# LSTM and three sign-weight layers on one core: more steps under the seven products, and low parts computed in pieces between the recurrence's instructions

## The chip, the core and the metric

One core of a Trainium2 chip. The metric is the device time of one execution in microseconds (us), median of several. TensorE multiplies into PSUM; ScalarE, VectorE and GpSimd do the elementwise work; SyncE and ScalarE issue the DMAs.

## The reference, cut to what matters

```python
# x (32, 64, 256): batch 32, 64 steps; h0 = cond_1024 (32, 256); c0 = 0
xW = x @ Wx + b                                   # (32, 64, 1024)
for t in range(64):
    a = xW[:, t] + h @ Wh                         # i, f, o, g of 256 each
    c = sigmoid(f) * c + sigmoid(i) * tanh(g)
    h = sigmoid(o) * tanh(c);  hs[:, t] = h
y = concatenate([hs, -hs], -1)
y = relu(s0 * (y @ sign(k0))) * 2                 # 512 -> 1024, weights +1 or -1
y = relu(s1 * (y @ sign(k1))) * 2                 # 1024 -> 1024
out = x + s2 * (y @ sign(k2))                     # 1024 -> 256
```

## The kernel before

Values are held transposed: features on the 128 partitions, steps times batch in columns. Precision comes from pairs: a value is a 16-bit high part and a 16-bit low part (value minus high part), and each product is two matmuls, one for each part.

**The recurrence.** In step t TensorE adds 16 matmuls of 32 columns (L512, high part of h) and 16 of 64 columns (L521, both parts) to the three gate sums. VectorE adds the halves (`add_halves`, L965: forget gate, then input gate and candidate, then output gate), ScalarE takes the tanh of each (L717), VectorE makes uT (L1063), vT (L1066), cD (L1069) and oP (L1071), ScalarE tanh of the cell (L834), and VectorE h's high part (L1075), h in 32 bits (L1076) and its low part hl (L1078). Between, ScalarE seeds the next step's gate sums from xw (L710). Each engine runs its instructions in program order.

**The filler.** All other matmuls are put by `make_plan` behind the gate matmuls of some step, in the order of `tile_order`, each step with a budget in us (`fill`). A tile is an output of 128 features: ("x", i, j) is input projection (six 512-column f32 matmuls, L542), (0, c, n) and (1, c, n) are tiles of the first and second layer for portion c (4 and 16 matmuls, L559), ("o", c, k) the third layer's four matmuls on the second layer's tile k (L592). `CHUNKS` gives portions as first step and number of steps, 32 columns a step: five of 8 and two of 12.

**Emptying a tile.** ScalarE writes the high part (`layer_hi`, L733) or, for x, adds the bias and stores to xw (`x_empty`, L701), behind the seeds of the next step (`act_plan`). VectorE writes the low part (`layer_lo`, L888), behind hl and ahead of the next step's gate sums (`dve_plan`). The planner counts them as emptied, and later matmuls really wait for the semaphores.

**The last two portions, N1 and N2,** share the second layer by Winograd's form of Strassen's algorithm: seven half-size products p1 to p7 of NW columns (L577) in place of eight, with sums of weights (`mix_part`, GpSimd, L1136) and of activations. For N1's first-layer tiles ScalarE writes a 32-bit copy r1 (L727) and then the high part (L733), and GpSimd the low part (`r1_rest`, L1156). p1 and p2 run within the steps; ScalarE empties them (`p1_copy` L738, `c11_hi` L743), VectorE writes p2's low part (`c11_lo`, L893). Behind the last step come N2's first layer with its four VectorE operations a block (`n2_terms`, L917 to L922), the third layer of portion N1 - 1 interleaved (`tail_order`), its two adds (L903), the third layer's first half for N1 (L612), which waits for these adds, then p3 to p7, and the remaining outputs, adds and stores. Splits of x into high and low parts sit in fixed steps (`X2_STEPS`, `X3_STEPS`; `x_hi` at L692).

The core of the planner's choice for VectorE:

```python
time = ahead + STEP + spent - CHAIN - KEEP - LOW * (t in W2_STEPS)
for x in todo:
    if len(now) < 2 or sum(map(vector_cost, now + [x])) <= time:
        now.append(x)
```

`todo` are finished tiles whose last matmul lies at least 0.75 us (planned) ahead of the step's end, and older ones.

Of the kernel before, what the change touches and what calls it, by code (L numbers as in the profile page):

```python
# [37 lines left out]
CHUNKS = ((0, 8), (8, 8), (16, 8), (24, 8), (32, 8), (40, 12), (52, 12))  # L38
N1, N2 = 5, 6
# [17 lines left out]
CHORES, EVICTIONS = 1.3, 1.7  # L57
# [41 lines left out]
def act_cost(tile):  # L99
    return 0.48 if tile[0] == "y" else 0.67 if tile[0] == "x" else 0.95 if tile[:2] == (0, N1) else 0.38  # L100


# [49 lines left out]
def make_plan():  # L152
# [124 lines left out]
    for tile, a in tail_order(rest):  # L277
# [7 lines left out]
        if a + 1 == matmuls(tile) and tile[0] in (0, 1, "p2", "p3", "p4", "p7"):  # L285
            free.append((bank[tile], tile))
            empty_at[tile] = at + 1.2
            if tile[0] == 0:
# [4 lines left out]


def lstm_ffn(nc, x_d, small_d, wx_d, wh_d, k0_d, k1_d, k2_d, out_d):
    ctx = ExitStack()
    with ctx:
# [918 lines left out]
```

## Time and profile before

| | |
|---|---|
| median of 3 runs | 272.74 us (272.41 to 273.35) |
| the profiled execution | 272.65 us, its span 270.7 us |
| TensorE busy | 266.5 us, 98% |
| VectorE busy | 219.5 us, 81% |
| ScalarE busy | 193.0 us, 71% |
| GpSimd busy | 48.2 us, 18% |
| granted TensorE clock | 0.999 |

A busy TensorE counts overlapping matmuls once; a listed duration of one matmul is longer than the distance to the next, so pitches are read from runs of equal matmuls in a row. Lines are numbered as in the kernel printed above; L559 and its like are the matmuls of the layers.

### The profile page before, as it was taken

The numbers are of one execution on the slowest core, as the hardware profiler recorded it, in microseconds if no ns is written. First come the engines' busy times: TensorE is split into PE (matmuls) and PEld (weight loads), VectorE is DVE, ScalarE is ACT, GpSimd is POOL, SyncE is SP. The second block draws the span as 40 slices with busy tenths as digits, with TensorE's granted clock in tenths as the row PEclk, the third lists the DMA queues.
The fourth block names the chain that finished last, engine by engine and source line by source line (L and its number), as shares of the span: only waits on it lengthen the run. The fifth ranks groups of instructions, "written<-read, shape, count | busy, mean of one in ns | idle before, by whom it ended". The sixth has DMA issues, their size and how long they took to land.

```text
span 270.7 us, 9163 instructions
## 1 busy us (share of the span) xinstructions
PE 266.5 (98%) x3568; PEld 220.0 (81%) x3568; DVE 219.5 (81%) x833; ACT 193.0 (71%) x650; POOL 48.2 (18%) x70
## 2 busy tenths in 40 slices
PE   8999999999999999999999999999999999999995
PEld 5877888888999999999999999998887777556663
DVE  3887888888888888888888888888887777998355
ACT  5799898989677768766867677667888976734320
POOL 0010000022211112331222102000222225603030
PEclk9999999999999999999999999999999999999999
DMA  6990000000000000000010001000000010100003
GB/s 208 325 366 2 2 2 0 2 4 2 4 2 1 2 2 22 23 4 4 2 42 0 2 4 42 2 2 2 4 1 2 2 42 0 41 0 0 2 0 116
DMA packets 5434, 8.74 MB, mean 32 GB/s; under 512 B 656, under 2 KB 3472, under 8 KB 5264
## 3 DMA queue, kind: packets, MB, share of 16 engines
q1 hardware_dynamic: 5104, 7.64, 8.1%
q8 instruction: 28, 0.46, 0.7%
q10 hardware_dynamic: 288, 0.52, 0.6%
q14 instruction: 14, 0.11, 0.1%
HBM read 6.07 MB, written 2.10 MB: 30 GB/s over the span
## 4 chain that ended last, share of the span: by engine, by line
PE 97%; DMA 1%; DVE 1%; issue 0%
PE WK L559 36%; PE WK L542 15%; PE G L521 11%; PE WK L577 10%; PE G L512 9%; PE ACC L592 6%; PE G L577 4%; PE WK L612 2%; PE G L542 2%; DMA x<-in_x 1%; DVE x L903 1%; PE G L612 1%; PE ACC L612 1%; PE ACC L542 1%; PE G L559 0%; DVE xs L1012 0%
## 5 line engine op out<-in xcount | busy, mean ns | idle before, releaser
L559 PE MATMUL WK<-h,k 128*128 128x256 f16 (+1 forms) x856 | 107.7, 276 | 0.0
L559 PEld LDWEIGHTS WK<-h,k 128*128 128x128 fp8e5 x856 | 80.8, 98 | 11.2
L717 ACT ACTIVATE tT<-aT 128x64 f32<-128x64 f32 x189 | 51.6, 274 | 42.6 <-DVE aT L965 31.2
L965 DVE TENSOR_REDUCE aT<-G 128x64 f32<-128x128 f32 (+1 forms) x192 | 59.4, 331 | 6.1 <-PE G L521 4.8
L710 ACT ACTIVATE G<-xw 128x256 f32<-128x256 f32 x189 | 52.3, 298 | 0.0
L542 PE MATMUL WK<-xs,wxs 128*128 128x512 f32 x168 | 42.6, 400 | 0.0
L521 PE MATMUL G<-h,w 128*128 128x64 f16 x1008 | 39.5, 192 | 0.0
L512 PEld LDWEIGHTS G<-h,w 128*128 128x128 f16 x1008 | 33.3, 96 | 5.8 <-DVE h L1075 3.1
L542 PEld LDWEIGHTS WK<-xs,wxs 128*128 128x128 f32 x168 | 30.4, 188 | 6.1 <-DVE xs L883 0.3
L512 PE MATMUL G<-h,w 128*128 128x32 f16 x1008 | 35.1, 176 | 0.0
L521 PEld LDWEIGHTS G<-h,w 128*128 128x128 f16 x1008 | 33.2, 97 | 0.0
L888 DVE SCALAR_TENSOR_TENSOR h<-WK,h 128x256 f16<-128x256 f32 x80 | 30.9, 418 | 1.2
L733 ACT ACTIVATE h<-WK 128x256 f16<-128x256 f32 x80 | 26.6, 367 | 0.1
L1075 DVE TENSOR_TENSOR h<-oP,tC 128x64 f16<-128x64 f32 x64 | 14.4, 225 | 14.1 <-ACT tC L834 14.0
L1136 POOL TENSOR_TENSOR mix<-k 128x256 fp8e5<-128x256 fp8e5 x16 | 10.3, 648 | 70.9 <-DVE h L1078 70.9
L592 PE MATMUL ACC<-h,k 128*128 128x256 f16 x160 | 22.0, 273 | 0.0
L1069 DVE SCALAR_TENSOR_TENSOR cD<-uT,vT 128x64 f32<-128x64 f32 x63 | 14.2, 225 | 6.6
L701 ACT ACTIVATE xw<-WK,biasS 128x512 f32<-128x512 f32 x28 | 18.0, 676 | 0.6 <-PE WK L542 0.6
L834 ACT ACTIVATE tC<-cD 128x64 f32<-128x64 f32 x64 | 16.4, 256 | 1.0 <-DVE cD L1069 0.3
L592 PEld LDWEIGHTS ACC<-h,k 128*128 128x128 fp8e5 x160 | 15.3, 98 | 2.1
L577 PE MATMUL WK<-xw,k 128*128 128x384 f16 x96 | 16.7, 326 | 0.0
L1078 DVE TENSOR_TENSOR h<-h 128x64 f16<-128x64 f32 x64 | 14.4, 225 | 2.2
(119 smaller groups left out, 287.3 us busy)
## 6 DMA issues: line engine op xcount, KB each, us to landing
x<-in_x SPq DMA_DIRECT2D x3, 512.0 KB, 8.7
out_y<-x SPq DMA_DIRECT2D x10, 128.0 KB, 1.8
xw<-in_wh SPq DMA_DIRECT2D x4, 256.0 KB, 4.9
k<-in_k SPq DMA_DIRECT2D x1, 1024.0 KB, 10.6
out_y<-x SPq DMA_DIRECT2D x4, 192.0 KB, 1.9
x<-in_x ACTq DMA_DIRECT2D x2, 256.0 KB, 3.6
xw<-in_wx SPq DMA_DIRECT2D x4, 128.0 KB, 3.8
xw<-in_wx SPq DMA_DIRECT2D x2, 256.0 KB, 5.1
```

Source lines behind the costliest of these rows:

```text
L512: eng.matmul(gate_sum(g, j)[:, 0:B], w16[:, 1, j, k], hi[:, k], start=False, stop=False, skip_group_check=True)
L521: ins = eng.matmul(gate_sum(g, j), w16[:, 0, j, k], pair[:, k].rearrange("p a b -> p (a b)"), start=False, stop=j == GATES[g][1] - 1 and k ...
L542: ins = eng.matmul(TILE[bank[tile]][:, :], wxs[:, wp, k, j], xs[:, i % 2, xp, k], start=a == 0, stop=a == 5)
L559: ins = eng.matmul(layer_src(tile), w, rhs, start=a == 0, stop=last)
L577: ins = eng.matmul(layer_src(tile), w[:, k, 128 * m:128 * m + 128], rhs[:, k, part], start=a == 0 and q not in (2, 6, 7), stop=a == 7, ski ...
L592: ins = eng.matmul(out_sum(c, mo), w2[:, k, 128 * mo:128 * mo + 128], h2[:, k, part, 0:width(tile)], start=k == 0 and a == 0, stop=k == 7 ...
L701: eng.activation(xw[:, 4 * i:4 * i + 4, j], TILE[bank[tile]][:, :].rearrange("p (u c) -> p u c", c=128), ACT.Identity, bias=biasS[:, j:j + ...
L710: eng.activation(G[g][:, 0:64 * (j1 - j0)].rearrange("p (j h b) -> p j h b", h=2, b=B), src.unsqueeze(2).broadcast_to((P, j1 - j0, 2, B)), ...
L717: eng.activation(tT[:, B * j0:B * j1], aT[:, j0:j1].rearrange("p j b -> p (j b)"), ACT.Tanh, scale=half_gain0 if t == 0 else half_gain).th ...
L733: eng.activation(layer_dst(tile, 0), layer_src(tile), ACT.Relu).then_inc(hi_made[layer])
L888: eng.scalar_tensor_tensor(layer_dst(tile, 1), layer_src(tile), 0.0, layer_dst(tile, 0), ALU.max, ALU.subtract).then_inc(lo_made[tile[0]])
L965: eng.tensor_reduce(aT[:, j0:j1], G[g][:, 0:64 * (j1 - j0)].rearrange("p (j h b) -> p j b h", h=2, b=B), op=ALU.add, axis=AX.X).then_inc(a ...
```

## The change

- `CHUNKS`: four portions of 8 steps and two of 16. The pair under the seven products covers steps 32 to 63 (it covered 40 to 63); NW is 512 instead of 384. N1 is now portion 4, the fifth.
- The budget `fill` is 2.06 us in every step from 1 on; at most 1.2 us of planned evictions (instead of 1.7) before an output copy is put off.
- `low` replaces `layer_lo` and `c11_lo` and takes a range of columns. In each step one older tile (`between_plan`) has columns 0 to 127 done ahead of cD, 128 to 255 ahead of h, and the rest, if any, behind hl. Behind hl one further tile is done, two when more than three are queued.
- `add_halves(t, O)` stands ahead of uT.
- N1's first-layer tiles: ScalarE copies only columns 256 to 511 to r1 (`r1_half`), then writes the high part of all 512; VectorE writes the low part of columns 0 to 255 (`low`); GpSimd writes the low part of 256 to 511 (`r1_rest`) and later adds high and low part of 0 to 255 to complete r1 (`r1_sum`).
- Four output tiles of portion N1 - 1 move from behind the last step to behind p1's first two tiles.
- Buffers: room of xs and wxs is used again for t23 and two of tq; semaphore waits go with it. Hunks with only these, renamed plans and constants of the bank choice behind the loop are left out below.

```diff
--- before.py
+++ after.py
...
-CHUNKS = ((0, 8), (8, 8), (16, 8), (24, 8), (32, 8), (40, 12), (52, 12))
-N1, N2 = 5, 6
+CHUNKS = ((0, 8), (8, 8), (16, 8), (24, 8), (32, 16), (48, 16))
+N1, N2 = 4, 5
 NW = B * CHUNKS[N1][1]
...
 MIX_STEP, MIXES = 10, 32
-CHORES, EVICTIONS = 1.3, 1.7
+CHORES, EVICTIONS = 1.3, 1.2
...
-    return 3.4 if t < 0 else 1.8 if t < 1 else 2.3 if t < 9 else 2.2 if t < 16 else 2.3
+    return 3.4 if t < 0 else 1.8 if t < 1 else 2.06
...
+def low_width(tile):
+    return 256 if tile[:2] == (0, N1) else width(tile)
 def matmuls(tile):
...
 def act_cost(tile):
-    return 0.48 if tile[0] == "y" else 0.67 if tile[0] == "x" else 0.95 if tile[:2] == (0, N1) else 0.38
+    return 0.48 if tile[0] == "y" else 1.03 if tile[:2] == (0, N1) else 0.38 if tile[0] in (0, 1) else 0.67
...
 def pool_cost(chore):
-    return {"mix": 0.65, "y": 0.74, 0: 0.93}[chore[0]]
+    return {"mix": 0.65, "y": 0.74, "lo": 0.65, "sum": 0.65}[chore[0]]
...
     def third(c, m):
-        at = (2, 2, 3, 4, 5, 6, 6, 7) if c == 0 else (0, 1, 2, 3, 4, 5, 6, 6) if c < N1 - 1 else (1, 2, 3, 4, 5, 6, 6, 7)
-        return [((0, c + 1, n), 4) for n in range(8) if at[n] == m]
+        at = (2, 2, 3, 4, 5, 6, 6, 7) if c == 0 else (0, 1, 2, 3, 4, 5, 6, 6) if c < N1 - 1 else (2, 3, 4, 4, 5, 6, 6, 7)
+        return [((0, c + 1, n), 4) for n in range(len(at)) if at[n] == m]
...
-    return order + [((f"p{q}", m), 8) for q, m in ((1, 0), (1, 1), (1, 2), (2, 0), (1, 3), (2, 1), (2, 2), (2, 3))]
+    for tile in (("p1", 0), ("p1", 1), ("p1", 2), ("p2", 0), ("p1", 3), ("p2", 1), ("p2", 2), ("p2", 3)):
+        order.append((tile, matmuls(tile)))
+        if tile[0] == "p1" and tile[1] < 2:
+            order += [(("o", N1 - 1, 2 * tile[1] + k), 4) for k in range(2)]
+    return order
...
-    others = outs(N1 - 1, *range(8))
+    others = outs(N1 - 1, *range(4, 8))
     order = left + others[:10]
...
-    pe, act, dve, pool = ([[] for _ in range(T + 2)] for _ in range(4))
+    pe, act, dve, pool, between = ([[] for _ in range(T + 2)] for _ in range(5))
     bank, before = {}, {}
...
         elif tile[0] == "p1":
-            inputs = (0, N1, a // 2) in paired
+            inputs = (0, N1, a // 2) in emptied and ("lo", a // 2) in paired
         elif tile[0] == "p2":
-            inputs = (0, N1, 4 + a // 2) in paired and ("p1", tile[1]) in emptied
+            inputs = (0, N1, 4 + a // 2) in emptied and ("lo", 4 + a // 2) in paired and ("p1", tile[1]) in emptied
         else:
...
         late, held = [], []
+        between[t], todo = todo[:1], todo[1:]
+        emptied.update(between[t])
         if MIX_STEP <= t < MIX_STEP + MIXES:
             chores.append(("mix", t - MIX_STEP))
-        chores.sort(key=lambda x: (x[0] != 0, x[0] == "mix"))
+        chores.sort(key=lambda x: ("lo", "y", "mix", "sum").index(x[0]))
         while chores and 0 <= t < T and sum(map(pool_cost, pool[t] + chores[:1])) <= CHORES:
...
         for tile, at in sorted(kept + finished, key=lambda x: x[0][0] == "y"):
-            if tile[0] in ("x", "p1", "y") or tile[:2] == (0, N1):
+            if tile[0] in ("x", "p1", "y"):
                 emptied.add(tile)
-            if tile[0] == "y" or tile[:2] == (0, N1):
+            if tile[0] == "y":
                 chores.append(tile)
...
-            time = ahead + STEP + spent - CHAIN - KEEP - LOW * (t in W2_STEPS)
-            now = []
-            for x in todo:
-                if len(now) < 2 or sum(map(vector_cost, now + [x])) <= time:
-                    now.append(x)
-            ahead += STEP + spent - max(CHAIN_MIN, CHAIN + sum(map(vector_cost, now)))
-            ahead = min(max(ahead, 0.0), AHEAD)
+            wide = any(low_width(tile) > 256 for tile in between[t])
+            now = todo[:2 if len(todo) + len(late) > 3 and t not in W2_STEPS else 1 - wide]
         act[t].sort(key=lambda x: (x[0] == "y", x[0] == "x"))
...
         emptied.update(now)
+        chores += [("lo", tile[2]) for tile in act[t] if tile[:2] == (0, N1)]
+        chores += [("sum", tile[2]) for tile in between[t] + now if tile[:2] == (0, N1)]
         todo = [x for x in todo if x not in now] + late
     dve[T] = todo
+    pool[T] = chores
...
                     e.wait_ge(r1_lo, 4 * (q - 1) + k + 1)
+                    e.wait_ge(r1_lo2, 4 * (q - 1) + k + 1)
                     e.wait_ge(w1_made, 2)
...
                 elif old[0] == 0 and old[1] == N1:
-                    e.wait_ge(hi_made[0], 8 * N1 + old[2] + 1)
+                    e.wait_ge(r1_lo, old[2] + 1)
+                    e.wait_ge(r1_half, old[2] + 1)
                 elif old[0] in (0, 1):
...
                     e.wait_ge(seeded[O], 32)
-                    eng.activation(r1[:, m], layer_src(tile), ACT.Relu).then_inc(r1_made)
+                    eng.activation(r1[:, m, 256:NW], layer_src(tile)[:, 256:NW], ACT.Relu).then_inc(r1_half)
                 if layer == 1 and c > 0:
...
-            def layer_lo(tile):
-                e.wait_ge(hi_made[tile[0]], 8 * tile[1] + tile[2] + 1)
-                eng.scalar_tensor_tensor(layer_dst(tile, 1), layer_src(tile), 0.0, layer_dst(tile, 0),
-                                         ALU.max, ALU.subtract).then_inc(lo_made[tile[0]])
-            def c11_lo(tile):
-                e.wait_ge(c_hi[11], tile[1] + 1)
-                eng.scalar_tensor_tensor(c11[:, tile[1], 1], layer_src(tile), 0.0, c11[:, tile[1], 0],
-                                         ALU.max, ALU.subtract).then_inc(c_lo[11])
+            def low(tile, c0, c1):
+                if tile[0] == "p2":
+                    hi, lo, src = c11[:, tile[1], 0], c11[:, tile[1], 1], layer_src(tile)
+                    e.wait_ge(c_hi[11], tile[1] + 1)
+                else:
+                    hi, lo, src = layer_dst(tile, 0), layer_dst(tile, 1), layer_src(tile)
+                    e.wait_ge(hi_made[tile[0]], 8 * tile[1] + tile[2] + 1)
+                ins = eng.scalar_tensor_tensor(lo[:, c0:c1], src[:, c0:c1], 0.0, hi[:, c0:c1], ALU.max, ALU.subtract)
+                if c1 == low_width(tile):
+                    ins.then_inc(c_lo[11] if tile[0] == "p2" else r1_lo if tile[:2] == (0, N1) else lo_made[tile[0]])
...
-            def empty(tile):
-                if tile[0] == "p2":
-                    c11_lo(tile)
-                else:
-                    layer_lo(tile)
             def n2_terms(k):
...
                 e.wait_ge(r1_made, k + 1)
+                e.wait_ge(r1_half, k + 1)
                 eng.scalar_tensor_tensor(t1f[:, k], b, 0.0, r1[:, k], ALU.max, ALU.subtract).then_inc(t_made[0])
...
                 else:
+                    add_halves(t, O)
                     e.wait_ge(tanhed[F], t + 1)
...
                     eng.scalar_tensor_tensor(uT[:, :], tf, 1.0, cD[:, :], ALU.add, ALU.mult).then_inc(u_made)
-                    add_halves(t, O)
                     e.wait_ge(tanhed[GI], t + 1)
                     eng.scalar_tensor_tensor(vT[:, :], ti, 1.0, tg, ALU.add, ALU.mult).then_inc(v_made)
+                    for tile in between_plan[t]:
+                        low(tile, 0, 128)
                     e.wait_ge(u_made, t)
...
                                   ALU.add).then_inc(o_made)
+                for tile in between_plan[t]:
+                    low(tile, 128, 256)
                 e.wait_ge(c_tanh, t + 1)
...
                 eng.tensor_tensor(h16[:, t, :, 1], h32[:, t % 2], h16[:, t, :, 0], ALU.subtract).then_inc(hl_made)
+                for tile in between_plan[t]:
+                    if low_width(tile) > 256:
+                        low(tile, 256, low_width(tile))
                 if t in X2_STEPS:
...
                 for tile in dve_plan[t]:
-                    empty(tile)
+                    low(tile, 0, low_width(tile))
             for tile in dve_plan[T]:
-                empty(tile)
+                low(tile, 0, low_width(tile))
             for mo in range(2):
...
-                eng.wait_ge(r1_made, m + 1)
+                eng.wait_ge(r1_half, m + 1)
                 eng.wait_ge(hi_made[0], 8 * N1 + m + 1)
-                eng.tensor_tensor(b1[:, m, 1], r1[:, m], b1[:, m, 0], ALU.subtract).then_inc(r1_lo)
+                eng.tensor_tensor(b1[:, m, 1, 256:NW], r1[:, m, 256:NW], b1[:, m, 0, 256:NW], ALU.subtract).then_inc(r1_lo2)
+            def r1_sum(m):
+                eng.wait_ge(r1_lo, m + 1)
+                eng.tensor_tensor(r1[:, m, 0:256], b1[:, m, 0, 0:256], b1[:, m, 1, 0:256], ALU.add).then_inc(r1_made)
...
                         y_add(chore[1], chore[2])
+                    elif chore[0] == "lo":
+                        r1_rest(chore[1])
                     else:
-                        r1_rest(chore[2])
+                        r1_sum(chore[1])
+            for chore in pool_plan[T]:
+                r1_sum(chore[1])
             for k in range(4):
```

## Rows read from the trace of the kernel before

**Rows 1.** The page: the chain that ended last, shares by engine.
```profile
PE 97%; DMA 1%; DVE 1%; issue 0%
```

**Rows 2.** Busy time of each engine from the first step to the end, sum of seven windows.
```profile
sum 251.57, PE 248.51 PEld 206.06 DVE 206.56 ACT 178.93 POOL 46.13; mean PE 35.50 PEld 29.44 DVE 29.51 ACT 25.56 POOL 6.59
```

**Rows 3.** The chain in order of time: start us, us, what, how many in a row.
```profile
42.75 2.39 PE WK L542 x10
137.90 2.40 PE WK L559 x22
239.04 10.40 PE WK L577 x64
```

**Rows 4.** Timeline of one step of the recurrence: start us, us, engine, line.
```profile
133.18 0.22 DVE L1075 TENSOR_TENSOR h<-oP,tC 128x64 f16<-128x64 f32 x1 [0.21 <-ACT tC L834]
133.45 0.64 ACT L733 ACTIVATE h<-WK 128x256 f16<-128x256 f32 x2
133.71 0.56 PE L512 MATMUL G<-h,w 128*128 128x32 f16 x16
133.71 0.75 DVE L888 SCALAR_TENSOR_TENSOR h<-WK,h 128x256 f16<-128x256 f32 x2
134.43 0.66 DVE L965 TENSOR_REDUCE aT<-G 128x64 f32<-128x128 f32 x2
134.57 2.46 PE L559 MATMUL WK<-h,k 128*128 128x256 f16 x21
134.75 1.00 ACT L717 ACTIVATE tT<-aT 128x64 f32<-128x64 f32 x3 [0.30 <-DVE aT L965]
135.46 0.22 DVE L1066 SCALAR_TENSOR_TENSOR vT<-tT 128x64 f32<-128x64 f32 x1
135.79 0.23 DVE L1069 SCALAR_TENSOR_TENSOR cD<-uT,vT 128x64 f32<-128x64 f32 x1
136.34 0.22 DVE L1075 TENSOR_TENSOR h<-oP,tC 128x64 f16<-128x64 f32 x1 [0.22 <-ACT tC L834]
```

**Rows 5.** Timeline of the third step's start, in the input-projection stretch.
```profile
25.02 0.61 ACT L692 ACTIVATE xs<-x 128x512 fp32r<-128x512 f32 x1
25.05 0.23 DVE L1075 TENSOR_TENSOR h<-oP,tC 128x64 f16<-128x64 f32 x1 [0.52 <-ACT tC L834]
25.33 0.57 PE L512 MATMUL G<-h,w 128*128 128x32 f16 x16
25.54 1.25 ACT L701 ACTIVATE xw<-WK,biasS 128x512 f32<-128x512 f32 x2
28.17 0.22 DVE L1075 TENSOR_TENSOR h<-oP,tC 128x64 f16<-128x64 f32 x1 [0.22 <-ACT tC L834]
```

**Rows 6.** Timeline of the last step.
```profile
219.73 0.55 PE L512 MATMUL G<-h,w 128*128 128x32 f16 x16
220.37 0.56 DVE L893 SCALAR_TENSOR_TENSOR h<-WK,h 128x384 f16<-128x384 f32 x1 [0.54 <-ACT h L743]
222.71 0.23 DVE L1075 TENSOR_TENSOR h<-oP,tC 128x64 f16<-128x64 f32 x1 [0.21 <-ACT tC L834]
```

**Rows 7.** Instructions by line and form: busy us, mean ns, idle before.
```profile
L733 ACT ACTIVATE h<-WK 128x256 f16<-128x256 f32 x80 | 26.6, 367 | 0.1
L733 ACT ACTIVATE xw<-WK 128x384 f16<-128x384 f32 x8 | 3.9, 486 | 0.0
```

**Rows 8.** One line's instructions: duration ns min/median/max; and GpSimd mixing.
```profile
L959 DVE SCALAR_TENSOR_TENSOR h<-h x8: 547/558/1191, 247.4 to 264.9; 128x384 f16<-128x384 f32 x8
L1136 POOL TENSOR_TENSOR mix<-k 128x256 fp8e5<-128x256 fp8e5 x16 | 10.3, 648 | 70.9 <-DVE h L1078 70.9
```

**Rows 9.** Timeline of the stretch behind the last step.
```profile
225.02 0.56 DVE L917 SCALAR_TENSOR_TENSOR t1f<-WK,xw 128x384 f32<-128x384 f32 x1 [0.76 <-ACT xw L771]
226.62 0.55 DVE L922 SCALAR_TENSOR_TENSOR xw<-WK,xw 128x384 f16<-128x384 f32 x1
230.06 0.88 DVE L903 SCALAR_TENSOR_TENSOR x<-ACC,sc,x 128x256 f32<-128x256 f32 x2 [0.71 <-PE ACC L592]
```

More of the change, by code:

```diff
@@ L288, in make_plan @@
             if tile[0] == 0:
-                empty_at[tile] = 1.6 + 2.2 * (tile[2] % 4) + (1.7 if tile[2] < 4 else 3.4)
+                empty_at[tile] = 1.6 + 2.8 * (tile[2] % 4) + (2.1 if tile[2] < 4 else 4.2)
     act[T] = [tile for tile, a in rest if a + 1 == matmuls(tile)]
     dve[T] += [tile for tile in act[T] if tile[0] != "p1"]
-    return pe, act, dve, pool, bank, before
+    return pe, act, dve, pool, between, bank, before
 def lstm_ffn(nc, x_d, small_d, wx_d, wh_d, k0_d, k1_d, k2_d, out_d):
@@ L307, in lstm_ffn @@
         x = sb("x", [P, 2, T * B], F32)
-        xs = sb("xs", [P, 2, 2, 2, 512], F32R)
-        wxs = sb("wxs", [P, 2, 2, NJ, 128], F32R)
+        with nc.sbuf_tensor("xs", [P, 2, 2, 2, 512], F32R) as xs, nc.sbuf_tensor("wxs", [P, 2, 2, NJ, 128], F32R) as wxs:
+            pass
+        t23 = sb("t23", [P, 2, 4, NW], F32)
+        tq01 = sb("tq01", [P, 2, 4, 2, NW], F16)
         small = sb("small", [P, 2 * B + NJ + 3], F32)
@@ L323, in lstm_ffn @@
         seven = sb("seven", [P, 1], U32)
-        h1 = sb("h1", [P, 2, 16 * NW], F16)
+        h1 = sb("h1", [P, 2, 16 * B * CHUNKS[0][1]], F16)
         h2 = sb("h2", [P, 8, 2, NW], F16)
@@ L363, in lstm_ffn @@
         r12 = cut(xflat, 20 * NW, 2, NW)
-        tq = cut(xflat[:, 22 * NW:38 * NW].bitcast(F16), 0, 4, 4, 2, NW)
-        b22 = cut(xflat[:, 38 * NW:42 * NW].bitcast(F16), 0, 4, 2, NW)
+        b22 = cut(xflat[:, 22 * NW:26 * NW].bitcast(F16), 0, 4, 2, NW)
+        tq = [tq01[:, 0], tq01[:, 1], cut(xflat[:, 26 * NW:30 * NW].bitcast(F16), 0, 4, 2, NW), b1[:, 0:4]]
         t4f = cut(w16[:, :].rearrange("p a j k c -> p (a j k c)").bitcast(F32), 0, 4, NW)
@@ L410, in lstm_ffn @@
         acc_mm, y_out, y_made = ([sem(f"{n}{mo}") for mo in range(2)] for n in ("acc_mm", "y_out", "y_made"))
-        mixed, r1_made, r1_lo, p1_made, n2_mm, r12_made, hi22, lo22 = (
-            sem(n) for n in ("mixed", "r1_made", "r1_lo", "p1_made", "n2_mm", "r12_made", "hi22", "lo22"))
+        mixed, r1_made, r1_half, r1_lo, r1_lo2, p1_made, n2_mm, r12_made, hi22, lo22 = (
+            sem(n) for n in ("mixed", "r1_made", "r1_half", "r1_lo", "r1_lo2", "p1_made", "n2_mm", "r12_made", "hi22", "lo22"))
         prod_mm = {q: sem(f"prod_mm{q}") for q in range(1, 8)}
@@ L418, in lstm_ffn @@
         fin_mm, fin_y = ({c: [sem(f"{n}{c}_{mo}") for mo in range(2)] for c in (N1 - 1, N1, N2)} for n in ("fin_mm", "fin_y"))
-        pe_plan, act_plan, dve_plan, pool_plan, bank, before = make_plan()
+        pe_plan, act_plan, dve_plan, pool_plan, between_plan, bank, before = make_plan()
         def layer_dst(tile, part):
@@ L438, in out_sum @@
             return TILE[bank["y", mo]] if c == N2 else (ACC, G[O])[mo] if c == N1 else ACC[:, 256 * mo:256 * mo + 256]
[L440 to L441 removed]
+        factors = {1: (a11, b1[:, 0:4]), 2: (a12, b1[:, 4:8]), 3: (mix[:, 3], b22), 4: (a22, tq[3]),
+                   5: (mix[:, 0], tq[0]), 6: (mix[:, 1], tq[1]), 7: (mix[:, 2], tq[2])}
         out_parts = {N1: (11, c11, 21, c21), N2: (12, c12, 22, c22)}
@@ L736, in p1_copy @@
                 e.wait_ge(prod_mm[1], tile[1] + 1)
-                e.wait_ge(seeded[O], 32)
+                e.wait_ge(seeded[O], 40)
                 eng.activation(p1s[:, tile[1]], layer_src(tile), ACT.Copy).then_inc(p1_made)
@@ L778, in term_hi @@
                 e.wait_ge(t_made[i], k + 1)
-                eng.activation(tq[:, i, k, 0], term(i, k), ACT.Copy).then_inc(t_hi[i])
+                if i < 2:
+                    e.wait_ge(x_mm, 4 * NJ)
+                elif i == 3:
+                    e.wait_ge(prod_mm[2], 4)
+                eng.activation(tq[i][:, k, 0], term(i, k), ACT.Copy).then_inc(t_hi[i])
             def p5_copy(m):
@@ L925, in term_lo @@
                 e.wait_ge(t_hi[i], k + 1)
-                eng.tensor_tensor(tq[:, i, k, 1], term(i, k), tq[:, i, k, 0], ALU.subtract).then_inc(t_lo[i])
+                eng.tensor_tensor(tq[i][:, k, 1], term(i, k), tq[i][:, k, 0], ALU.subtract).then_inc(t_lo[i])
             def q_sum(m):
@@ L1139, in term_lo @@
                 eng.wait_ge(t_hi[i], k + 1)
-                eng.tensor_tensor(tq[:, i, k, 1], term(i, k), tq[:, i, k, 0], ALU.subtract).then_inc(t_lo[i])
+                eng.tensor_tensor(tq[i][:, k, 1], term(i, k), tq[i][:, k, 0], ALU.subtract).then_inc(t_lo[i])
             def term4(k):
@@ L1144, in term4 @@
                 eng.wait_ge(r1_made, 4 + k + 1)
+                eng.wait_ge(r1_half, 4 + k + 1)
                 eng.tensor_tensor(t4f[:, k], r1[:, 4 + k], t23[:, 0, k], ALU.subtract).then_inc(t_made[3])
```

5 lines of the change are left out of this document (1 added, 4 removed).

## The prediction

> **What bounds the kernel now.** I read four views in this order. The chain that ended last says who sets the end: TensorE, 97% of it [rows 1]. The table of windows says whether TensorE ever rests: from the first step's matmuls to the end it is busy 248.51 of 251.57 us [rows 2], and the 3 us missing lie behind its last matmul. So each matmul saved is time saved, as long as nothing else comes up to TensorE. The chain in order of time gives the true pitch of matmuls (their listed durations overlap): ten input-projection matmuls take 2.39 us, 0.239 each; 22 matmuls of 256 columns 2.40, 0.109 each; 64 of 384 columns 10.40, 0.1625 each [rows 3]. Last, the timeline of one step shows what comes up next. This is the decisive view, and the reader should see two clocks in it [rows 4].
>
> TensorE's clock: the gate matmuls take from 133.71 to 134.57, about 0.87 with the hand-over, then the filler; with 21 matmuls of 256 columns that is 0.87 + 21 x 0.109 = 3.16 us a step. The recurrence's clock: from the first gate matmul (133.71) to the next h (VectorE, L1075, 136.34) is 2.63 us; and from h to the first gate matmul that waits for it 25.33 - 25.05 = 0.28 [rows 5]. A step can't be shorter than 2.63 + 0.28 = 2.91. Now h starts at 133.18 and TensorE takes it up at 133.71, 0.53 later where 0.28 would do: 0.25 us of slack in every step, which hides whatever ScalarE or VectorE do too late.
>
> **The change, part by part.** The sum is made on the profiled execution, 272.65 us.
>
> Matmuls (-2.2). Layers one and three stay as large; layer two costs 4096 columns a step of the sequence when done plainly (8 tiles x 16 matmuls x 32) and 7/8 of it, 3584, in the seven products. Eight more steps fall under the products: 8 x 512 = 4096 columns. The pitches of 256 and 384 columns differ by 0.0534, so 0.417 ns a column: 1.7 us. The same line puts 512 columns at 0.216. In full: before 960 x 0.109 + 352 x 0.1625 = 161.8; after 768 x 0.109 + 352 x 0.216 = 159.7. With the digits kept that is 2.2; bounds 1.7 (columns only) and 2.3.
>
> Fill. The loop's filler budget falls from 2.2 or 2.3 to 2.06 us a step; what it leaves goes behind the loop (57 us of planned matmuls there instead of 45), where nothing waits for a recurrence. With 19 matmuls of 256 columns a step is 0.87 + 2.07 = 2.94 us. The floor is 2.91. The slack of 0.25 becomes 0.03, and every lateness that [rows 4] hides is now to be paid. All terms below are of this kind.
>
> Halves of low parts between (0). A low part of 256 columns is now two of 128, one ahead of cD and one ahead of h. Two full ones take 0.75 and the second alone 0.42, so each occupies VectorE 0.33, and 128 columns fewer 0.20. vT starts 135.46, cD 135.79: cD waits for vT's write, 0.33 later. vT occupies about 0.13 of it (its 0.22 less the 0.09 by which instructions overlap), so 0.20 fits to within 0.01. Ahead of h, VectorE idles 0.22 for ScalarE [rows 4]; the second half fits as well. The output reduction moved ahead of uT fills time in which vT waits for the tanh anyway. I take 0; if the fit fails it is at most the length of a half's tail, 0.06, in some 33 steps: 2.0 us.
>
> Input-projection steps (+0.9). A step now holds nine such matmuls: 0.87 + 9 x 0.239 = 3.02, slack 0.11. ScalarE's evictions follow each other by about 0.6 (two take 1.25), the split of x by 0.52 [rows 5]. They start 0.27 behind h (133.45 - 133.18) and the forget gate's tanh is due 1.04 behind the gate matmuls, 1.32 behind h without slack [rows 4]. Nine matmuls complete one and two tiles in turn, and of the four steps that also split x (0, 1, 3, 4) steps 1 and 3 get two. The trace has one such load, split and two tiles, with no slack ahead: the next h came 28.17 - 25.33 = 2.84 behind the gates, 0.21 late, although ScalarE had started 0.30 early (25.02 with h at 25.05, not 0.27 behind it). Started normally it is 0.51 late; less the slack, 0.40, and against 3.02 the step loses 2.91 + 0.40 - 3.02 = 0.29. Two of them, 0.6. The h at 25.05 itself waited 0.52 instead of 0.22 [rows 5], for no reason that I can read; ten matmuls covered it, nine don't: 0.3 more if it comes again. Bounds 0.3 and 1.3.
>
> Granularity (+0.2). Filler comes in pieces of 0.216 and 0.239, so some steps get under 2.04 and then run at 2.91. Bounds 0 and 0.6.
>
> The first paired portion's tiles (+1.8), the fifth portion now, the sixth before. VectorE had nothing to do with them: ScalarE wrote both the copy and the high part and GpSimd the low. Now VectorE makes the low part of columns 0 to 255, and where a tile ends early in a step, in that same step, behind hl and ahead of the next gate reduction. It must wait for ScalarE, whose order is the copy of half the tile, then the high part of all 512 columns. Durations: 0.367 at 256 columns, 0.486 at 384, so 0.605 at 512; pitch of the first 0.28 [rows 7]. High part ready at 0.27 + 0.28 + 0.60 = 1.15 behind h, low part on to 1.51, and the reduction was due at 134.43 - 133.71 = 0.72 behind the gates, 1.00 behind h. 0.51 late, less 0.06 of slack: 0.45. The last step of before shows exactly this wait, with a tile of 384: VectorE idles 0.54 for ScalarE and h comes 222.71 - 219.73 = 2.98 behind the gates, not 2.63, with 0.23 of slack used up [rows 6]. How often? I laid the order against the budget: the fourth portion's second layer, with which these tiles are interleaved, starts in step 46, and counting 2.06 a step from there, tiles 0, 3 and 6 of the eight end early with no older tile queued (about steps 49, 52, 55); the others queue behind another tile or go between. Of the four second products, 512 wide on VectorE, one does so (it would be 0.50 late). Four times 0.45. Bounds 0.4 and 3.6.
>
> GpSimd (+0.3). It gains eight sums; a step may hold a low half and a sum. One 256-column operation takes 0.64, so two end 0.69 + 1.28 = 1.97 behind h; uT must start by 1.9. A VectorE operation on two SBUF operands went from 547 to 1191 ns beside GpSimd [rows 8]. If that holds for uT, some 0.1 in a few steps: 0.3, bounds 0 and 1.0. The Trainium skill, SBUF — State Buffer, "Who interferes with whom", says that a VectorE instruction with two SBUF inputs and a GpSimd one that reads SBUF exclude each other for the whole instruction. The trace agrees as far as that 1191 goes. By the rule the sum stays where it is or rises to rival (d); without it, it would be 0.3 lower.
>
> Behind the loop (+0.5, +0.2). Sixteen output matmuls were moved into the loop, so TensorE now reaches the outputs that need ACC emptied sooner, while VectorE's four terms a block get longer: three pitches were 226.62 - 225.02 = 1.60, at 512 columns 2.00, and 2.6 a block. Counted from the first output matmul behind the loop: first tile at 10 x 0.109 + 4 x 0.216 = 1.95, ScalarE's copy with its start to 2.75, first term at 2.95; the block takes 2.6 (5.55), the next one stands ready and takes it to 8.2, two adds (0.88) to 9.1 [rows 9]. TensorE: 10 x 0.109 + 32 x 0.216 + 6 x 0.109 = 8.65. It waits 0.5; bounds 0 and 1.0. The last add is 0.13 wider and its store a third larger: 0.2. The products' later sums scale no more than the matmuls that cover them.
>
> Sum: 272.65 - 2.2 + 0.9 + 0.2 + 1.8 + 0.3 + 0.5 + 0.2 = 274.35. The median of before stands 0.09 above its profiled run: 274.4.
>
> **Rivals.** (a) TensorE stays the bound, on the faster side: the early tiles find an older one queued, the split steps are as cheap as they were, and only the two terms behind the loop and a little remain: 272.74 - 2.2 + 0.7 = 271.2. It decides if the waits of all steps together stay under some 0.7 us, which is no more than one early tile and one split step. For it: 2.94 is above 2.91. Against it: the wait in the last step of before [rows 6]. 0.25. (b) Half of the waits: total 1.4 to 3.0 above the matmul term, 272 to 273.5, no measurable change: 0.2. (c) The halves push cD in every plain step: 274.4 + 33 x 0.06 = 276.4, all steps from 16 to 48 at 3.0 instead of 2.94. 0.12. (d) The rule on the shared ports taken at its hardest, all eight sums each holding uT back by 0.16: 1.3 instead of 0.3, 275.4: 0.08. My forecast, 273.6 to 275.4, has 0.35.
>
> **The numbers.** Slower holds (c), (d) and the forecast: 0.55; same 0.2; faster 0.25. What a measurement can tell from no change is 0.3%, 0.8 us. Cases of both signs hold much, so the range runs from (a), a little under it, to above (c): 271.0 to 277.0; the forecast's own is 273.6 to 275.4.
>
> **What would show it.** Plain steps 16 to 45 at 2.94 us with h 2.63 to 2.66 behind the gates; 3.0 or more means (c). Steps 2 and 4 near 3.3. In steps 49 to 62 a few of 3.3 to 3.4 with VectorE idle for ScalarE's high part; none means (a). A gap of half a microsecond on TensorE ahead of the fifth portion's outputs. 512-column matmuls at 0.216; were they at 0.22, the first term would be 1.4 us smaller and the forecast wrong from its start.

## The result, and the profile after

The changed kernel takes 275.13 us (median of 5 runs, 274.69 to 275.69); before, in runs on the same chip, 272.95 (272.41 to 273.37). The ratio is 1.0082, 95% interval 1.0068 to 1.0095: 0.8% slower. The profiled execution took 275.69 us with a span of 273.7, where before had 272.65 and 270.7. Lines have moved: the gate matmuls are L521 (32 columns) and L530 (64), input projection L551, layers L568, products L587, outputs L602 and L622; ScalarE's tanh L728, high part L744, r1's half L738; VectorE's low part L909, reduction L977, uT L1076, vT L1078, cD L1083, h L1091, output adds L920.

The page of the kernel after:

```profile
span 273.7 us, 8789 instructions
...
PE 267.2 (98%) x3376; PEld 199.1 (73%) x3376; DVE 222.7 (81%) x860; ACT 186.1 (68%) x632; POOL 52.7 (19%) x76
...
PE 69%; DVE 17%; ACT 9%; issue 3%; DVEq 0%; POOL 0%; ACTq 0%; POOLq 0%
```

TensorE is as busy as before, 98%, yet the chain that ended last lies on it for 69% instead of 97% [rows 1]. Of the other 31%, about 27 lie in the steps: stretches in which some step's h comes just late enough to matter, so that the chain runs back through VectorE and ScalarE. Some 3 lie behind the last step, where the chain runs through VectorE's terms and output adds. Seen alone, the busy share would have hidden the change entirely.

The windows of the kernel after, from the first gate matmul to the last h and from there to the end (busy us of each engine and number of instructions, granted clock, DMA share, GB/s), answer to [rows 2]:

```profile
19.91:212.45 192.54, 190.80 (x3026) 157.97 (x3026) 165.76 (x755) 148.02 (x566) 35.25 (x54) 1.00 0.02 7
212.45:273.70 61.25, 57.50 (x274) 26.48 (x272) 43.75 (x67) 24.20 (x42) 15.46 (x12) 0.99 0.06 22
```

The granted clock is 1.00 and 0.99, the upper of its two levels (2.4 GHz); it falls to 0.50 only at 272.7, when the last matmul (270.4) is over, so the clock explains nothing. The listed busy time runs over small gaps, because listed matmuls overlap, so I counted the waits by step instead: the period of a step (from one first gate matmul to the next), less 0.868 us of gate matmuls, less its filler matmuls at their pitches (0.109, 0.216 and 0.239 us here). TensorE's idle time in steps 0 to 62 so counted is 3.63 us; the same count gave 0.13 for the kernel before.

The account of the two profiled executions, us of span: matmuls -2.13 (in the loop -14.64, behind it +12.51); idle in the loop +3.50; a wait ahead of the outputs that need ACC +0.57; from the last matmul's end, at its pitch, to the end +0.28 (3.46 instead of 3.18); start of the first step +0.78 (19.91 instead of 19.13, a weight load that landed later). Sum +3.00, measured 3.0. The last term isn't the change's: over the profiles of all ten kernels here the first step starts between 18.93 and 19.91 in no relation that I can see to their edits. Without it 2.2 is left, and the medians differ by 2.18.

From the chain in order of time, kernel after (start us, us, what, how many in a row):

```profile
231.94 12.52 PE WK L587 x58
```

58 matmuls of 512 columns in 12.52 us are 0.216 each; 256 columns still take 0.109.

A plain step, kernel after (timeline):

```profile
144.09 0.21 DVE L1076 SCALAR_TENSOR_TENSOR uT<-tT,cD 128x64 f32<-128x64 f32 x1
144.35 0.23 DVE L1078 SCALAR_TENSOR_TENSOR vT<-tT 128x64 f32<-128x64 f32 x1
...
144.49 0.28 DVE L909 SCALAR_TENSOR_TENSOR h<-WK,h 128x128 f16<-128x128 f32 x1
144.69 0.22 DVE L1083 SCALAR_TENSOR_TENSOR cD<-uT,vT 128x64 f32<-128x64 f32 x1
144.83 0.19 DVE L1085 TENSOR_SCALAR oP<-tT 128x64 f32<-128x64 f32 x1
144.93 0.28 DVE L909 SCALAR_TENSOR_TENSOR h<-WK,h 128x128 f16<-128x128 f32 x1
...
145.23 0.23 DVE L1091 TENSOR_TENSOR h<-oP,tC 128x64 f16<-128x64 f32 x1
...
145.54 0.56 PE L521 MATMUL G<-h,w 128*128 128x32 f16 x16
```

Two halves of a low part lie among the recurrence's instructions, cD comes 0.34 behind vT (0.33 in [rows 4]), and h to the next gate matmul is 0.31. From the gates to h it is 2.63 us in nearly every step from 18 to 41, and the period is 2.94.

The steps that lost something, by the same count: step 1 0.31, 4 0.22, 9 0.27, 16 0.29, 42 1.17, 53 0.31, 56 0.42, 61 0.13, and -0.06 to 0.12 in the others (the slightly negative ones mix input projection and layers, for which the pitches are not exact). Step 42 and the one behind it, TensorE of the kernel after:

```profile
145.54 0.56 PE L521 MATMUL G<-h,w 128*128 128x32 f16 x16
145.95 0.63 PE L530 MATMUL G<-h,w 128*128 128x64 f16 x16
146.41 1.04 PE L568 MATMUL WK<-h,k 128*128 128x256 f16 x8
148.45 0.56 PE L521 MATMUL G<-h,w 128*128 128x32 f16 x16 [1.01 <-DVE h L1091]
148.87 0.63 PE L530 MATMUL G<-h,w 128*128 128x64 f16 x16
149.33 1.04 PE L602 MATMUL ACC<-h,k 128*128 128x256 f16 x8
150.20 2.35 PE L568 MATMUL WK<-h,k 128*128 128x256 f16 x20
152.39 0.55 PE L521 MATMUL G<-h,w 128*128 128x32 f16 x16
```

Eight filler matmuls in one step, 28 in the next, which so takes 3.94 us. No engine was late: h at 148.17 is 2.63 behind the gates. The planner had nothing that it allowed itself to place. The second portion's output is copied out of ACC in two pieces (0.48 us planned each, ScalarE, L774). The first runs in step 38, at 134.00. The second, with the two high parts (0.38 each) that each of the next four steps has, makes 1.24 us of planned evictions, over the limit of 1.2; so it is put off from step to step and runs in step 43, at 148.71. Until then the third layer's next tiles (L602), which need ACC empty, can't be placed, and in step 42 everything else is queued behind them.

Step 53, kernel after. A tile of the first paired portion (the fifth now) has ended early in the step ahead, so VectorE takes its low part behind that step's h and ahead of this step's reduction:

```profile
178.80 0.36 ACT L738 ACTIVATE xw<-WK 128x256 f32<-128x256 f32 x1
...
178.93 0.55 PE L521 MATMUL G<-h,w 128*128 128x32 f16 x16
179.06 0.58 ACT L744 ACTIVATE xw<-WK 128x512 f16<-128x512 f32 x1
...
179.68 0.42 DVE L909 SCALAR_TENSOR_TENSOR xw<-WK,xw 128x256 f16<-128x256 f32 x1 [0.53 <-ACT xw L744]
...
180.02 0.81 DVE L977 TENSOR_REDUCE aT<-G 128x64 f32<-128x128 f32 x3
180.33 0.79 ACT L728 ACTIVATE tT<-aT 128x64 f32<-128x64 f32 x3 [0.69 <-DVE aT L977]
180.75 0.21 DVE L1076 SCALAR_TENSOR_TENSOR uT<-tT,cD 128x64 f32<-128x64 f32 x1
...
181.89 0.23 DVE L1091 TENSOR_TENSOR h<-oP,tC 128x64 f16<-128x64 f32 x1 [0.22 <-ACT tC L849]
```

VectorE waits 0.53 us for the high part, the reduction starts 1.09 behind the gates instead of 0.72, and h comes 2.96 behind the gates. GpSimd's sum (L1181) of this step ran from 179.85 to 180.52, so it was over before uT.

The waits of TensorE, kernel after (us in total, times, longest), and the place of the second one in the timeline:

```profile
PE G L521 <- DVE h L1091: 1.4, 3, 1.0
...
PE ACC L622 <- DVE x L920: 0.4, 1, 0.4
...
218.69 2.75 PE L568 MATMUL WK<-h,k 128*128 128x512 f16 x12
...
221.85 0.59 PE L622 MATMUL ACC<-h,k 128*128 128x512 f16 x2 [0.40 <-DVE x L920]
```

The list counts only gaps between listed, overlapping durations. For the gate matmuls it has 1.4 us, less than half of the 3.63: waits of 0.3 us don't show in such a list, they show in the periods. The wait for VectorE's output adds (L920) is listed with 0.40, but twelve matmuls of 0.216 from 218.69 end at 221.28, and the outputs start at 221.85: TensorE lost 0.57.

### The profile page after: what moved, and what is told of

The parts are those of the page before. It is cut to its first block, busy times and chain, and to the rows that moved or that the text cites. A ratio compares the mean times of both kernels' runs of the same rounds, so it can differ in the third digit from the quotient of the medians.

```text
span 273.7 us, 8789 instructions
## 1 busy us (share of the span) xinstructions
PE 267.2 (98%) x3376; PEld 199.1 (73%) x3376; DVE 222.7 (81%) x860; ACT 186.1 (68%) x632; POOL 52.7 (19%) x76
## 4 chain that ended last, share of the span: by engine, by line
PE 69%; DVE 17%; ACT 9%; issue 3%; DVEq 0%; POOL 0%; ACTq 0%; POOLq 0%
PE WK L568 18%; PE WK L587 13%; PE G L530 7%; PE WK L551 7%; PE G L521 6%; PE ACC L602 5%; DVE aT L977 5%; PE G L587 4%; PE WK L622 3%; ACT tT L728 3%; ACT G L721 2%; DVE cD L1083 2%; DVE h L909 2%; DVE vT L1078 2%; PE G L551 2%
## 5 line engine op out<-in xcount | busy, mean ns | idle before, releaser
L568 PE MATMUL WK<-h,k 128*128 128x256 f16 (+1 forms) x696 | 92.0, 281 | 0.0
L568 PEld LDWEIGHTS WK<-h,k 128*128 128x128 fp8e5 x696 | 65.1, 98 | 12.0
L728 ACT ACTIVATE tT<-aT 128x64 f32<-128x64 f32 x189 | 44.7, 268 | 29.7 <-DVE aT L977 22.7
L977 DVE TENSOR_REDUCE aT<-G 128x64 f32<-128x128 f32 (+1 forms) x192 | 54.2, 331 | 8.0 <-PE G L530 7.7
L551 PE MATMUL WK<-xs,wxs 128*128 128x512 f32 x168 | 42.9, 400 | 0.0
L521 PEld LDWEIGHTS G<-h,w 128*128 128x128 f16 x1008 | 30.4, 96 | 13.4 <-DVE h L1091 10.6
L530 PE MATMUL G<-h,w 128*128 128x64 f16 x1008 | 39.5, 192 | 0.0
L521 PE MATMUL G<-h,w 128*128 128x32 f16 x1008 | 35.2, 177 | 1.7 <-DVE h L1091 1.4
L909 DVE SCALAR_TENSOR_TENSOR h<-WK,h 128x128 f16<-128x128 f32 (+2 forms) x97 | 33.9, 351 | 2.0 <-ACT h L754 0.3
L551 PEld LDWEIGHTS WK<-xs,wxs 128*128 128x128 f32 x168 | 30.4, 188 | 5.7
L530 PEld LDWEIGHTS G<-h,w 128*128 128x128 f16 x1008 | 33.2, 97 | 0.0
L744 ACT ACTIVATE h<-WK 128x256 f16<-128x256 f32 x64 | 21.4, 367 | 1.1 <-PE WK L568 1.0
L1091 DVE TENSOR_TENSOR h<-oP,tC 128x64 f16<-128x64 f32 x64 | 14.4, 225 | 7.7 <-ACT tC L849 7.1
L587 PE MATMUL WK<-xw,k 128*128 128x512 f16 x80 | 19.1, 379 | 0.0
L602 PE MATMUL ACC<-h,k 128*128 128x256 f16 x128 | 17.9, 273 | 0.0
L1078 DVE SCALAR_TENSOR_TENSOR vT<-tT 128x64 f32<-128x64 f32 x63 | 14.2, 225 | 2.6
L1083 DVE SCALAR_TENSOR_TENSOR cD<-uT,vT 128x64 f32<-128x64 f32 x63 | 13.9, 220 | 3.0
```

Of the source, the lines that this page charges most:

```text
L521: eng.matmul(gate_sum(g, j)[:, 0:B], w16[:, 1, j, k], hi[:, k], start=False, stop=False, skip_group_check=True)
L530: ins = eng.matmul(gate_sum(g, j), w16[:, 0, j, k], pair[:, k].rearrange("p a b -> p (a b)"), start=False, stop=j == GATES[g][1] - 1 and k ...
L551: ins = eng.matmul(TILE[bank[tile]][:, :], wxs[:, wp, k, j], xs[:, i % 2, xp, k], start=a == 0, stop=a == 5)
L568: ins = eng.matmul(layer_src(tile), w, rhs, start=a == 0, stop=last)
L587: ins = eng.matmul(layer_src(tile), w[:, k, 128 * m:128 * m + 128], rhs[:, k, part], start=a == 0 and q not in (2, 6, 7), stop=a == 7, ski ...
L602: ins = eng.matmul(out_sum(c, mo), w2[:, k, 128 * mo:128 * mo + 128], h2[:, k, part, 0:width(tile)], start=k == 0 and a == 0, stop=k == 7 ...
```

## The experiments

Eight kernels. Idle time in the loop is counted as above. Ratios are against the kernel before on the same chip.

**The limit of planned evictions alone** (changed kernel):

```diff
-CHORES, EVICTIONS = 1.3, 1.2
+CHORES, EVICTIONS = 1.3, 1.25
```

> The changed kernel with one constant: the limit above which an output copy is put off goes from 1.2 to 1.25 us, so that two evictions and a copy (2 x 0.38 + 0.48 = 1.24) fit into one step. Theory: the limit is what emptied step 42 (8 filler matmuls, then TensorE idle 1.17 us of a step of 2.91), because the copy of the second portion's output came two steps late and the third portion's outputs could not be placed. Then step 42 has 19 matmuls and takes 2.94, step 43 takes 2.94 instead of 3.94, and the total falls by 1.0 to 1.2 us, to a ratio of about 1.004 to the kernel before. Rival: the copy in the earlier step makes the forget gate's tanh late by as much as it saves (up to 0.3 us) or TensorE waits there for another reason: total within 0.5 us of the changed kernel, 1.007 to 1.009.

Measured: 274.57 us, ratio 1.0056 (1.0036 to 1.0075). TensorE in the same stretch:

```profile
145.44 1.04 PE L568 MATMUL WK<-h,k 128*128 128x256 f16 x8
146.31 1.04 PE L602 MATMUL ACC<-h,k 128*128 128x256 f16 x8
147.18 0.49 PE L568 MATMUL WK<-h,k 128*128 128x256 f16 x3
147.51 0.56 PE L521 MATMUL G<-h,w 128*128 128x32 f16 x16
```

Nineteen matmuls in step 42 instead of eight, and both steps take 2.94. The second output copy now runs in step 39, at 136.23. But everything behind it runs earlier, and four steps now have an h that comes 2.95 to 3.08 behind the gates: 50 loses 0.41, 53 0.43, 56 as much as before, 61 0.42. Loop idle falls only from 3.63 to 3.14. In steps 50, 53, 56 and 61 VectorE waits for ScalarE's high part (0.54, 0.54, 0.54 and 0.26 us). So closing the hole removed its 1.17 in full, and 0.68 of that was paid again, because the order behind it moved and more tiles of the paired portions were taken in the step in which they end.

**The paired tiles not taken in the step in which they end:**

```diff
+            fresh = {tile for tile, _ in finished if low_width(tile) > 256 or tile[:2] == (0, N1)}
+            ripe = [x for x in todo if x not in fresh]
-            now = todo[:2 if len(todo) + len(late) > 3 and t not in W2_STEPS else 1 - wide]
+            now = ripe[:2 if len(todo) + len(late) > 3 and t not in W2_STEPS else 1 - wide]
```

> The changed kernel, but a paired portion's tile that ends in a step is never taken by VectorE in that same step behind hl; it goes between the next step's instructions. Theory (the prediction's largest term): VectorE waits there for ScalarE's 512-column high part; steps 53, 56 and 63, whose h comes 2.96, 3.06 and 3.07 us behind the gate matmuls, fall to 2.63 to 2.70, TensorE's idle time there (0.31 and 0.42, and what the last step delays) goes, and the total falls by 0.7 to 0.9 us, ratio about 1.005. Rival: ScalarE's own evictions (0.28 + 0.60 and more) make the tanh late by themselves, h stays at 2.9 or more and the time at 1.007 to 1.009.

Measured: 274.0 us, ratio 1.0033 (1.0014 to 1.0052). The timeline of step 53 (here L523 is the 32-column gate matmul, L746 the high part, L979 the reduction, L1093 h):

```profile
178.80 0.56 PE L523 MATMUL G<-h,w 128*128 128x32 f16 x16
178.93 0.58 ACT L746 ACTIVATE xw<-WK 128x512 f16<-128x512 f32 x1
...
179.52 0.85 DVE L979 TENSOR_REDUCE aT<-G 128x64 f32<-128x128 f32 x3 [0.51 <-PE G L532]
...
180.70 0.28 DVE L911 SCALAR_TENSOR_TENSOR xw<-WK,xw 128x128 f16<-128x128 f32 x1
...
181.13 0.28 DVE L911 SCALAR_TENSOR_TENSOR xw<-WK,xw 128x128 f16<-128x128 f32 x1
...
181.43 0.23 DVE L1093 TENSOR_TENSOR h<-oP,tC 128x64 f16<-128x64 f32 x1
```

The low part has gone into the gaps between the recurrence's instructions, the reduction waits for TensorE again, h comes 2.63 behind the gates, and steps 53 and 56 take 2.93 and 2.92. Step 42 still loses 1.17. Loop idle is 2.74: 0.9 less for these tiles.

**Both together.**

> The changed kernel with the first two edits together: the limit of 1.25 and no early tile of the paired portions. Alone, the limit gave about 0.6 us of the 1.17 and the early tiles 1.1. Theory: the limit's edit moved the later steps' filler by 11 matmuls, so that tiles 1, 4, 6 and a product were now early instead of 3, 6 and a product; with no early tiles at all both gains are whole: idle time of TensorE in the steps near 1.6 us instead of 3.6, ratio about 1.000. Rival: the rest of the first edit's gain went elsewhere (ScalarE late in step 40 or 41), then 1.002 to 1.003.

Measured: 273.15 us, ratio 1.0014 (1.0003 to 1.0024), loop idle 1.62. The gap to the changed kernel's ratio, 1.0082 - 1.0014 = 0.68%, is 1.9 us of the 2.18; the limit alone gave 0.26% and the tiles alone 0.49%. These ratios are good to about 0.2% each and can't tell whether the gains simply add up. The traces can: alone the edits take 0.49 and 0.89 off the loop idle, together 2.01, because the early tiles in which the first edit had paid 0.68 are gone as well. The hole's 1.17 and the tiles' 0.89 make 2.06.

**No halves between:**

```diff
-        between[t], todo = todo[:1], todo[1:]
...
-            now = todo[:2 if len(todo) + len(late) > 3 and t not in W2_STEPS else 1 - wide]
+            now = todo[:2]
```

> The changed kernel without low parts between the recurrence's instructions: all are whole and behind hl, up to two in a step. It undoes one part. Theory: the halves cost nothing where they are, and two whole ones behind hl end 1.19 us behind h where the reduction is due at 1.00, so a step with two tiles is 0.15 to 0.2 longer: plain steps of 3.1 instead of 2.94 in some 25 to 30 of the steps, total 3 to 6 us more, ratio 1.02 to 1.03. Rival (c) of the prediction, that the halves push the recurrence as much as whole ones do: no change, 1.006 to 1.010.

Measured: 280.88 us, ratio 1.0278 (1.0237 to 1.032). Loop idle 9.25. A step of it (L908 is the low part, L1090 h), and its chain shares:

```profile
80.35 0.56 PE L520 MATMUL G<-h,w 128*128 128x32 f16 x16
...
80.58 0.74 DVE L908 SCALAR_TENSOR_TENSOR h<-WK,h 128x256 f16<-128x256 f32 x2
...
81.24 0.81 DVE L976 TENSOR_REDUCE aT<-G 128x64 f32<-128x128 f32 x3
...
83.11 0.23 DVE L1090 TENSOR_TENSOR h<-oP,tC 128x64 f16<-128x64 f32 x1 [0.22 <-ACT tC L848]
```

```profile
PE 51%; DVE 27%; ACT 13%; issue 6%; DMA 1%; DVEq 0%; ACTq 0%
```

Two whole low parts ahead of the reduction make it start 0.89 behind the gates, where a plain step of the changed kernel has 0.72, and h comes at 2.76 (other steps, 31 for one, have 1.06 and 2.93; why they are later still wasn't looked into). Of the 31 steps from 20 to 50, 21 have a period of 3.03 or more. The halves are what makes 2.94 us reachable.

**The halves alone, in the kernel before,** with its portions, its budget and its matmuls; the output reduction ahead of uT goes with them.

> The kernel before with one part of the change alone: one older tile's low part goes in halves ahead of cD and ahead of h, and the output gate's reduction stands ahead of uT. Portions, budget and the way of the paired tiles are those of before, so the steps have their slack of 0.25 us. Theory: the part neither costs nor gains where there is slack, h 2.63 behind the gates and 0.53 ahead of the next ones: ratio 0.998 to 1.002. Rival: 860 instead of 833 VectorE instructions and more semaphore waits cost by themselves: 1.003 or more.

Measured: 273.24 us, ratio 1.0007 (0.9994 to 1.002): no change, with 851 VectorE instructions (I had expected 860). h 2.63 behind the gates, and TensorE takes it up 0.53 later, as before. The chain lies on TensorE for 89%, because its loop idle is 0.31; 0.22 of that is in step 19, where cD comes 0.70 behind vT with no half between them. The halves neither cost nor gain where 0.25 us of slack stand around.

**The steps with a split of x or a weight preparation:**

```diff
-X3_STEPS, W0_STEPS, W1_STEPS = (4, 5), (0, 3, 6), (7, 8)
+X3_STEPS, W0_STEPS, W1_STEPS = (5, 7), (0, 3, 4), (6, 8)
```

> The changed kernel with only the splits of x of the third group of steps moved to steps 5 and 7, where only one tile is emptied in the step before, and the preparation of the first two layers' weights moved with them. Theory: step 4, whose h comes 2.96 behind the gates, falls to 2.64 and its period from 3.24 to 3.05, and nothing else moves: 0.2 us, ratio 1.006 to 1.008. Rival: the cause is not the split; step 4 stays near 3.2.

Measured: 275.1 us, ratio 1.0081 (1.0066 to 1.0096), as the changed kernel. In the trace step 4 falls from 3.24 to 3.04 with h at 2.64, step 9 loses 0.20 instead of 0.27, and loop idle is 3.39 instead of 3.63. So the mechanism is there and is worth 0.2 to 0.3 us, which the times don't resolve.

**The output adds behind the loop one block earlier:** `y_add(N1 - 1, mo)` stands behind block k = 0 instead of k = 1.

> The changed kernel with only the two adds of the fourth portion's outputs behind the first block of the last portion's terms instead of the second. Theory: TensorE's wait of 0.40 us ahead of the first outputs that need ACC goes, and the terms, 0.9 us later, are still in time for p3's last block: 0.4 us, ratio 1.005 to 1.007. Rival: the later terms hold up p3 or the banks of the last portion's tiles, and as much is lost there: 1.008.

Measured: 274.71 us, ratio 1.007 (1.0054 to 1.0085). TensorE there:

```profile
217.71 2.75 PE L568 MATMUL WK<-h,k 128*128 128x512 f16 x12
220.30 0.59 PE L622 MATMUL ACC<-h,k 128*128 128x512 f16 x2
```

The wait for L920 is gone from the list: the outputs start a pitch behind the layer's last matmul. The loop is unchanged (189.47 us from the first step to the last, 189.46 before the edit), and from the last step's first gate matmul to the last matmul's listed end it is 60.42 instead of 60.98 us: the trace shows the wait's 0.57 gained, to within 0.01, and nothing lost to the later terms. The medians differ by 0.4, in the same direction, but the intervals overlap.

**All four edits together.**

> Four edits to the changed kernel together: the limit of 1.25, no early tile of the paired portions, the splits of x for the third group of steps in steps 5 and 7 instead of 4 and 5 (so that none meets two tiles; the preparation of weights moves with them), and the two adds of the fourth portion behind the first block of terms instead of the second. Theory: TensorE's idle times are each a wait of their own and add up: 1.1 + 0.8 + 0.2 + 0.4 = 2.5 us, total 272.6, ratio 0.996 to 1.001. Rival: each removed wait only uncovers another (two evictions a step, moved weight preparation), and less than half is gained: 1.004 or more.

Measured: 272.39 us (12 runs), ratio 0.997 (0.9952 to 0.9987): 0.3% faster than the kernel before, and 1.1% faster than the changed one. From its page:

```profile
span 270.6 us, 8792 instructions
...
PE 81%; DVE 9%; DMA 3%; ACT 2%; SPq 2%; issue 1%; POOL 0%; DVEq 0%
```

Loop idle is 1.41 us (steps 1 0.29, 9 0.18, 16 0.29, 61 0.18, the rest 0.12 or less). It is the fastest kernel of this study.

## Why the prediction was right, and where its terms were not

The forecast's mechanism is what happened: 2.1 us of matmuls were saved, and more than that was paid because the slack fell from 0.25 to 0.03 us. Point by point:

- **Matmuls, -2.2.** -2.13. The 512-column pitch came out at the 0.216 that the line through 256 and 384 gave.
- **Fill and halves, 0.** Right. Plain steps take 2.94 with h at 2.63, so rival (c), 3.0 us, fell; the halves alone change nothing measurable, and taking them out costs 2%.
- **Input-projection steps, +0.9.** 0.53. Step 4 lost 0.22 where I had 0.29, as the mechanism says, and moving its split gave it back. Step 2 lost nothing: h came at 2.72 and the period, 3.01, was the matmuls' own. The odd wait came again, at the same instruction (the last row below), and cost 0.31 in step 1, as priced.
- **Granularity, +0.2.** 0.31, in steps 58, 60 and 62.
- **Early paired tiles, +1.8.** This is the term that failed most. The mechanism is exact (waiting 0.53, see step 53), but it occurred in steps 53 and 56 alone with 0.31 and 0.42, 0.73 in all (for the tiles that end in steps 52 and 55, as laid out). The one that I had placed in step 49 queued behind an older one. One second product does it in the last step, h 3.07 behind the gates, but there eleven matmuls of 512 columns cover the wait, and removing it left the distance from step 63 to the last outputs' wait at 12.47 us in both kernels. The unit price was nearly right: the reduction began 1.49 and 1.50 behind the h before it, where I had 1.51. Step 53 was cheaper than 0.45 because the step ahead of it held more filler, so that its gates started 0.40 behind h instead of 0.28.
- **GpSimd, +0.3.** Nothing in the time, but not for want of a meeting. In steps 52, 54, 55, 57 and 58 the sum (L1181) still runs when uT (L1076) starts. Step 55:

```profile
186.15 0.66 POOL L1181 TENSOR_TENSOR xw<-xw 128x256 f32<-128x256 f16 x1
...
186.60 0.29 DVE L1076 SCALAR_TENSOR_TENSOR uT<-tT,cD 128x64 f32<-128x64 f32 x1
```

  In the first four uT is listed with 0.28 to 0.30 us, against a median of 0.215, and ends 0.08 behind the sum's end each time; in step 58 only 0.10 of the sum is left, and uT is no longer than usual. The Trainium skill, SBUF — State Buffer, "Who interferes with whom", says that a VectorE instruction with two SBUF inputs, as uT is, and a GpSimd one that reads SBUF, as the sum is, shut each other out. The trace agrees: in the ten profiles of this case no uT that starts beside a GpSimd instruction ends less than 0.08 behind that instruction's end. But uT is held by some 0.08 us, not by rival (d)'s 0.16, and that is hidden, since vT starts 0.26 behind uT's start as in every plain step; h stays at 2.63 to 2.65. So rival (d) fell on its price, and my 0.3 with it.
- **Behind the loop, +0.5 and +0.2.** The wait for ACC was 0.57, with the releaser that I had named. The tail was 0.28 longer.
- **What had no term.** Step 42, 1.17 us, half of the loss in the medians; steps 16 and 9, 0.29 and 0.27; steps 61 and 19, 0.13 and 0.06, where h came 2.88 and 2.73 behind the gates. In step 16 the planner had only 15 matmuls, in step 9 the weight preparation on VectorE (L1015, 0.81 us from 47.86) pushed the reduction to 48.58.

So the total, 274.4 against 275.13, owes much to luck. The loop terms summed to 3.2 and 3.50 were measured, but 1.74 of mine was not there (1.07 of early tiles, 0.37 of input projection, 0.3 of GpSimd), and 2.03 of what was measured I hadn't seen. What I missed was in the diff. The limit of 1.7 became 1.2 beside costs of 0.38 and 0.48, and 2 x 0.38 + 0.48 = 1.24. I costed the filler as a mean per step and never asked whether the planner could deliver it in every step. With a slack of 0.03 us the mean is no longer what counts.

What stays open: why the profiled execution of the changed kernel began 0.8 us later than that of before, since the starts vary without visible relation to the edits; and what makes the odd waits in steps 1 and 61. The losses of steps 9 and 16 are read from the trace; no run removed them.

## What to carry to other kernels

When a change trims a period until two engines' clocks nearly meet, cost it by each step's worst case and not by averages: a planner's threshold that skips one copy (1.24 against 1.2) cost more than half of what the arithmetic saved. Where a tile's emptying needs two engines in turn, leave it for the step behind and fill the second engine's gaps with pieces of it; that cost nothing measurable here and made a 2.94 us step possible. An engine 98% busy in both kernels told nothing; the chain's share (97% to 69%) and the period of each step told it all.

## What the hardware showed unasked

One h in the second step waited about 0.3 us longer than the others, at the same place in all ten kernels. The timeline of the kernel after:

```profile
25.14 0.19 DVE L1085 TENSOR_SCALAR oP<-tT 128x64 f32<-128x64 f32 x1
25.25 0.26 ACT L849 ACTIVATE tC<-cD 128x64 f32<-128x64 f32 x1 [0.20 <-DVE cD L1083]
...
25.85 0.23 DVE L1091 TENSOR_TENSOR h<-oP,tC 128x64 f16<-128x64 f32 x1 [0.53 <-ACT tC L849]
```

Its input stands ready at 25.51; in a step without halves h follows it within 0.04. In the kernel before the same h shows 0.52 [rows 5]. Two more such waits stand elsewhere: h of step 61 in the kernel after starts at 206.17, 0.27 behind its input, and step 19 of the halves alone has the late cD named above. A packet of a queue that loads instructions starts at 25.57 here, and at 25.01 in the kernel before, where h is late until 25.05. But such packets run through the whole execution, most of them beside no wait. That a load of VectorE's instructions causes the wait is a guess; no run tested it.

A low part of 128 columns is listed with 0.28 us but holds VectorE for 0.20 (144.49 to 144.69), since instructions overlap by some 0.08: the listed time of small instructions overstates what room they need.
